# A decoder of twelve layers: zero products added to TensorE's stream in cross attention and linear attention

## The reference, cut to what matters

```python
def _L0_xattn_ref(query, key, value, attention_bias, Wq, Wk, Wv, Wo):   # key = value = context, 77 tokens
    ...                                        # 16 heads of 16 features
    scores = jnp.einsum('bhqd,bhkd->bhqk', q, k) / np.sqrt(HEAD_DIM)
    ...                                        # plus the bias of each key, softmax over the 77 keys
    out = jnp.einsum('bhqk,bhkd->bhqd', probs, v)
    ...                                        # joined heads times Wo

def _L3_attn_ref(x, Wq, bq, Wk, bk, Wv, bv, Wc, We, Wo, bo, gamma, beta):
    q = x @ Wq + bq
    k = (x @ Wk + bk) @ Wc @ We                # 4 key heads, each repeated for 4 query heads
    v = (x @ Wv + bv) @ Wc @ We
    qf, kf = elu(q) + 1, elu(k) + 1
    kv_cum = jnp.cumsum(jnp.einsum('bhsf,bhsd->bhsfd', kf, v), axis=2)
    num = jnp.einsum('bhsf,bhsfd->bhsd', qf, kv_cum)
    den = jnp.einsum('bhsf,bhsf->bhs', qf, jnp.cumsum(kf, axis=2))[..., None] + EPS
    y = x + (num / den) @ Wo + bo
    ...                                        # layer norm of y, times gamma, plus beta
```

## Time and profile before

| | us |
|---|---|
| median of 3 runs | 11147.57 |
| the three runs | 11145.72 to 11165.72 |
| the profiled execution | 11157.64 |
| its span, first to last instruction | 11155.5 |
| PE busy in the span | 8653.4 (78%) |
| DVE busy | 6076.7 (54%) |
| ACT busy | 4464.0 (40%) |
| mean granted clock of TensorE | 0.843 |

### The profile page before, as it was taken

One profiled execution on the slowest core, in us unless ns is written; L12 is line 12 of the kernel. 1 busy time (PEld: TensorE's weight loads), 2 busy tenths in 40 slices (PEclk: granted clock), 3 DMA queues, 4 the chain that ended last, 5 costly groups with the idle time before them and its releaser, 6 DMA issues. The chain is left out here.

```text
span 11155.5 us, 122278 instructions
## 1 busy us (share of the span) xinstructions
PE 8653.4 (78%) x42558; PEld 4737.6 (42%) x42670; DVE 6076.7 (54%) x11571; ACT 4464.0 (40%) x7824; POOL 1932.4 (17%) x1926
## 2 busy tenths in 40 slices
PE   4887575957889798989878788788786899566665
PEld 1222253532333366456434344444343444345454
DVE  6777331026777365266239678755444565455553
ACT  3666131113555464155127456542111444233332
POOL 1100102020111011011001001100000100366666
PEclk8888667977999899999978789788776999778787
DMA  2321322112222000000000000000001322355556
GB/s 63 51 43 22 58 68 72 61 42 37 39 39 39 16 1 10 0 13 1 9 13 1 1 1 1 1 10 0 5 0 23 58 42 42 109 174 177 175 175 180
DMA packets 243487, 521.55 MB, mean 47 GB/s; under 512 B 55051, under 2 KB 94837, under 8 KB 241431
## 3 DMA queue, kind: packets, MB, share of 16 engines
q1 hardware_dynamic: 154887, 232.49, 10.4%
q0 software_dynamic: 88064, 282.15, 8.5%
HBM read 425.31 MB, written 75.53 MB: 45 GB/s over the span
## 5 line engine op out<-in xcount | busy, mean ns | idle before, releaser
L818 ACT ACTIVATE probs<-scores 128x1024 f32<-128x1024 f32 (+4 forms) x960 | 868.8, 937 | 892.7 <-PE scores L695 630.0
L907 DVE TENSOR_REDUCE row_max<-ring 128x1 f32<-128x512 f32 (+3 forms) x1792 | 1024.8, 625 | 246.9 <-PE ring L669 218.1
L3332 POOL DMA_INDIRECT r_got<-in_L_ffn_tables,r_pick_now x960 | 945.3, 985 | 424.4 <-issue 280.9
L695 PE MATMUL scores<-query_stack,key_stack 99*128 99x512 bf16 (+3 forms) x2816 | 850.9, 393 | 162.1 <-DVE levels L929 77.7
L3428 PE MATMUL r_psum_y<-r_diagonal,r_got 128*128 128x128 f32 x4096 | 648.7, 334 | 420.6 <-ACT r_diagonal L3475 420.6
L715 PE MATMUL outputs<-probs,head_values 128*32 128x512 f32 (+3 forms) x5632 | 781.2, 629 | 102.5 <-ACT probs L815 99.8
L3428 PEld LDWEIGHTS r_psum_y<-r_diagonal,r_got 128*128 128x128 f32 x4096 | 630.2, 247 | 489.0 <-ACT r_diagonal L3475 484.8
L815 ACT ACTIVATE probs<-levels,quant 128x1024 f32<-128x1024 uint8 x512 | 612.7, 1234 | 328.5 <-DVE levels L929 325.2
L929 DVE TENSOR_SCALAR levels<-scores 128x1024 uint8<-128x1024 f32 x512 | 607.4, 1219 | 178.4 <-PE scores L695 146.3
L669 PE MATMUL ring<-key_stack,query_stack 96*128 96x512 bf16 (+3 forms) x1792 | 608.7, 382 | 65.1 <-DMA key_stack<-normed_parts 41.2
L3253 DVE TENSOR_TENSOR_SCAN state<-decay,added 128x1024 f32<-128x1024 f32 x256 | 583.4, 2279 | 33.4 <-ACT decay L3227 33.0
(11 more groups left out here) (597 smaller groups left out, 15551.2 us busy)
## 6 DMA issues: line engine op xcount, KB each, us to landing
joined_heads<-heads_out SPq DMA_DIRECT2D x512, 32.0 KB, 2.0
expert_w<-in_L_ffn_w SPq DMA_DIRECT2D x16, 1024.0 KB, 10.8
r_got<-in_L_ffn_tables,r_pick_now POOLq DMA_INDIRECT x960, 3.7
quant_parts<-parts SPq DMA_DIRECT2D x48, 256.0 KB, 5.1
query_stack<-quant_parts SPq DMA_DIRECT2D x48, 256.0 KB, 8.6
key_stack<-quant_parts SPq DMA_DIRECT2D x48, 256.0 KB, 8.0
query_stack<-cross_parts SPq DMA_DIRECT2D x48, 256.0 KB, 8.3
normed_parts<-parts SPq DMA_DIRECT2D x48, 256.0 KB, 5.3
```

The lines of the kernel that those rows point to most:

```text
L695: last = nc.tensor.matmul(out[:, off:GROUP], keys, q_stack[0:rows, h, half * GROUP + off:(half + 1) * GROUP], start=True, stop=not edge)
L818: nc.scalar.activation(dst, s_ps[0:k_rows, 2 * (e % 2):2 * (e % 2) + 2, off:GROUP], ACT.Exp, scale=scale).then_inc(probs_ready, 1)
L907: nc.vector.reduce_max(row_max[:, i, qt, at:at + 1], src[:, 0:cols], AX.X).then_inc(ring_read, 1)
L3332: nc.gpsimd.indirect_dma_start(out=b["got"][:, n, :], out_offset=None, in_=b["tables"], in_offset=bass.IndirectOffsetOnAxis(ap=b[picks][:, ...
```

## The change

Both stages get a tile of zeros in bfloat16, 128 by 512, set by DVE in the stage's set-up step, and PE gets extra products (`fill`) with the bfloat16 identity as the stationary operand and the zeros as the moving one. Their results, zeros, are read by nobody and overwritten later.

In cross attention `ring_bank` issues two fills before its wait. The stationary operand is 32 columns of the identity, and the result goes to partitions 96 to 127 of the first scores bank, which scores never use. In linear attention the stationary operand is the whole identity. From round 2 on, `products` issues a fill before its third and one before its fourth product, into the spread bank that this round's sums will use, from round 4 on after a wait for `out_done` of the chunk that used it before. `outputs` issues one into the outputs bank before it waits for the state. `sums` issues one into its spread bank, and the wait for `raw_ready` moves behind it.

```diff
+FILLED = 96
...
+        filler = sb("cross_filler", [P, GROUP], BF16)
...
-                dve.wait_ge(set_, 3)
+                nc.vector.memset(filler[:, :], 0.0).then_inc(set_, 1)
+                dve.wait_ge(set_, 4)
...
+                def fill():
+                    nc.tensor.matmul(s_ps[FILLED:P, 0, :], chip.id_bf[:, 0:P - FILLED], filler[:, :], start=True, stop=True)
+
                 def ring_bank(step_):
                     r = ring[step_]
+                    fill()
+                    fill()
                     if r >= 3:
                         pe.wait_ge(ring_read, r - 2)
...
+        filler = ctx.enter_context(sbuf(nc, "linear_filler", [P, GROUP], BF16))
...
+                nc.vector.memset(filler[:, :], 0.0).then_inc(set_, 1)
...
+                def fill(bank):
+                    nc.tensor.matmul(bank, chip.id_bf[:, :], filler[:, :], start=True, stop=True)
+
                 def products(c):
                     for g in range(KV_HEADS):
                         n = KV_HEADS * c + g
+                        if c >= 2 and g >= 2:
+                            if c >= 4:
+                                pe.wait_ge(out_done, c - 3)
+                            fill(spread_ps[:, c % 2, :])
                         if n >= 3:
                             pe.wait_ge(masked_ready, n - 2)
...
                 def outputs(c):
                     if c >= 2:
                         pe.wait_ge(raw_ready, c - 1)
+                    fill(out_ps[:, c % 2, :])
...
                 def sums(c):
-                    pe.wait_ge(raw_ready, c + 1)
                     if c >= 2:
                         pe.wait_ge(out_done, c - 1)
+                    fill(spread_ps[:, c % 2, :])
+                    pe.wait_ge(raw_ready, c + 1)
```

More of the change, by code:

```diff
@@ L1635, in _ @@
                 nc.vector.memset(v_rows[:, :, :, HEAD:HEAD + 1], 1.0).then_inc(set_, 1)
-                dve.wait_ge(set_, 4)
+                dve.wait_ge(set_, 5)
         with nc.Fori(0, BATCH) as b:
             linear_features(chip, b, wq, bq, wkv, bkv, wc, wk, wkv_up, q_f, k_f, k_rows, v_rows)
-            linear_chunks(chip, q_f, k_f, k_rows, v_rows, ot)
+            linear_chunks(chip, q_f, k_f, k_rows, v_rows, ot, filler)
             with banks(nc, "norm_psum", [P, 8, GROUP], F32) as norm_ps:
@@ L1736, in _, with linear_chunks @@
                                                    op0=ALU.add, op1=ALU.max).then_inc(features_ready, 1)
-def linear_chunks(chip, q_f, k_f, k_rows, v_rows, ot):
+def linear_chunks(chip, q_f, k_f, k_rows, v_rows, ot, filler):
     nc = chip.nc
```

## The result

The changed kernel took 11199.06 us (median of 7 runs, 11175.44 to 11204.26) against 11147.57 us before (median of 7, 11137.93 to 11165.72): ratio 1.0039, 95% interval 1.0027 to 1.0050, about 51 us slower. The forecast was slower by 136 us, 11284. The direction holds, the size is less than half of it, and the steps behind the size were wrong.

The account below looks back on a forecast made before the run. PE, often granted less than its full clock, was taken to set the pace in cross attention. Cross +180 and linear -44 gave +136 us on 11157.6, 11294, or 11284 for the lower run median; range 11100 to 11400.

Parts of the forecast that it names:

- Slower, and in cross attention: Cross attention: PE sets the pace, 512 fills mostly push back what follows, 15 of 93 idle us vanish; stage +180 us.
- They use a quarter of the array ... so they thin out what raises it: Cross attention: fills of 128 rows by 32 columns hold the clock less well, mean 0.64 for 0.68 to 0.70.
- The price of a fill, 0.22 us fast: Cross attention: each fill adds 0.22 us at 2.4 GHz, 0.43 slow; 512 of them cost 113 us fast, 220 slow.
- all fast: Both stages: any product keeps the clock at 2.4 GHz; cross +2 us, linear saves 56, total 11094; chance 0.10.
- Linear, -44 forecast: Linear attention: chunks take 8.2 us on the mean, 7.8 at 2.4 GHz, saving 11 us per batch, 44 in four.
- falls for one stretch ... in every third or so: Linear chunks: clock stays up through most, drops for 3.4 us in every third or so; 0.4 us more per chunk.
- The new wait for out_done costs nothing: Linear products, in front of the first fill: DVE's product ends before products 0 and 1 do; no cost fast or slow.
- No effect on the clock: Both stages keep their present clock despite the fills: +137 us cross, +36 linear, total 11321; chance 0.13.
- pinned slow: Cross attention: clock stays at 1.2 GHz throughout, +318 us, linear still saves 44, total 11422; chance 0.07.
- Beside: Cross attention: fills run concurrently with neighbouring products on their own array columns; stage +4 us, total 11108; chance 0.05.
- Hidden: Cross attention: PE's 93 idle us take in what fills they can, leaving +61 us; total 11165; chance 0.08.

## Why the prediction was wrong

- **Slower, and in cross attention: right.** PE set the pace, most fills were not hidden. PE's idle time fell from 93 to 64 us, by 29 where 15 were forecast.
- **"They use a quarter of the array ... so they thin out what raises it": wrong, and the main error.** I weighed a fill by rows times columns. The clock went up to 0.91, not down to 0.64. At 32 columns, fills of 32 rows in place of 128 lost it (0.58 against 0.90); at 128 rows, 128 columns in place of 32 added nothing (0.89 against 0.90). So a quarter of the array in all its rows held the clock as well as the whole. Whether it is the rows alone that count stays open: a fill of 32 by 32 is also thinner by area than one of 128 by 32 (a sixteenth of the array, a quarter), and no run has 32 rows with 128 columns. The earlier trace rows could not part rows from area: four products of 77 rows side by side on 32 columns each are thin by rows as well as by area (1297.3 to 1300.7), and the linear products of 16 rows likewise.
- **The price of a fill, 0.22 us fast: mis-sized.** It measured 0.30 (388.65 x 0.91 = 354 us, less 203, by 512; an estimate, busy time by mean clock), since each pair between products of other widths pays twice for the change; 151 us at full clock, not 113. My row was scores following scores, with no change of width in it. With the right price and the forecast clock it would have come out far above: 354/0.64 + 64 = 617 us. With my price at the measured clock, 316/0.91 + 64 = 411. The measured 453 is 354/0.91 + 64. So the two errors pulled opposite ways. With the clock alone put right, my sum would have been 411 - 392 - 44 = -25, faster: that the direction came out right is in part luck. The rival "all fast" failed by its price, not by its clock: it had 394 us.
- **The Trainium skill's rule** that the gate follows how busy PE has been recently (TensorE: Matmul & The Clock Gate, Part 1, "What's actually happening") came nearer for these fills than my weighing did. Taken as bare busy time it is too coarse: with 32-row fills PE was busy for 587 of 632 us at 0.58.
- **Linear, -44 forecast, -4 measured.** A fast chunk took 8.39 us for the 7.8 summed: with the third product parted from the first two, the phases of products follow each other at 1.37 us with their fill (7999.14, 8000.52, 8001.89), not at 1.1. A phase takes 1.05 us up to the fill behind it, not 0.88, and a fill in front of one 0.32, not 0.22. And the fall that I priced at 0.4 us per chunk came more often and lasted longer: 12.85 us for the next chunk, clock 0.74 for the above 0.85 that was to be seen. The step that failed is "falls for one stretch ... in every third or so". In the settled chunk of 10.04 us it costs 1.65 us over the fast 8.39; of the 1.8 us over my 8.2 some 0.6 are the fast chunk's and 1.2 the clock's. Leaving products 0 to 2 together removes the first and most of the second, and gives the 7.55 us per chunk; the 61 us saved are about what the bound "all fast" (56) had. That the place of these two fills is the cause is shown by that run.
- **The new wait for out_done costs nothing: right for the most part.** Over the first batch's chunks, of who waited for whom (us in total, times, longest):

```profile
PEld linear_spread L1772 <- DVE linear_out L1867: 3.2, 4, 1.0
...
PE linear_spread L1772 <- DVE linear_out L1867: 0.8, 1, 0.8
```

PE itself waited for it once, its weight loads four times, under running products or at the batch's tail. The fill of the chunk at 8007.53, whose weight load is put down to it, starts 1.07 us after the products as in the chunk before (1.06).

- **Same and other rivals.** "No effect on the clock" and "pinned slow" are out by the clock of 0.91, and ones did no more than zeros. "Beside" is out: even next to scores of 77 columns the fill starts after them and adds the change (0.53 us behind 1453.61). "Hidden" is out: PE's idle time fell by 29 us, with 151 us of fills at full clock.

## What to carry to other kernels

A filler is worth its place only where the engine would idle anyway: in linear attention two fills in an existing 0.77 us wait, with the real products left side by side, made the stage 9% shorter, and the same four fills per chunk, one of them parting the third product from the first two, made it under 1% shorter. Give a filler all 128 rows and the width of its neighbours, which is what did best here, and price it by a row with the same neighbours. In this stage, whose engine was 76% busy, filler cost more than the clock gave back in each of the five ways tried.

## What the runs showed of the hardware that I had not expected

Fills that use a quarter of the array, in all its rows, held the clock as well as whole ones: 512 fills of 128 rows by 32 columns 0.90, of 128 by 128 columns 0.89. Of 32 rows by 32 columns they lowered it to 0.58, under the 0.70 without fills. A pair of bfloat16 fills of 512 columns costs 0.43 us between products of its own width and 0.63 between others. Half as many fills gave not half the rise but a fifth (0.70 without, 0.74, 0.90), so the stage with 256 fills was no faster than the one with 512 (464 and 457 us).
